# A fused transformer layer in fp32: the output projection's offset added in the second norm, and VectorE's loop end in attention set behind a pair's maxima

## What is computed

```python
x = _ln(src) * (1.0 + scale) + shift
q = (x @ Wq + bq) ... ; k = (x @ Wk + bk) ... ; v = (x @ Wv + bv) ...
scores = jnp.einsum('bhqd,bhkd->bhqk', q / math.sqrt(HEAD_DIM), k) + attention_bias
scores = jnp.where(src_mask, -jnp.inf, scores)
probs = jax.nn.softmax(scores, axis=-1)
ctx = jnp.einsum('bhqk,bhkd->bhqd', probs, v).transpose(0, 2, 1, 3).reshape(B, S, D)
x = x + (ctx @ Wo + bo)
h = _ln(x) * g2 + beta2
ff = _gelu2(h @ W1 + b1) @ W2 + b2
return x + ff
```

## Time and profile before

| | |
|---|---|
| median of 3 runs | 2465.89 us (2464.13 to 2466.8) |
| the profiled execution | 2472.93 us, its span 2471.1 us |
| mean granted TensorE clock | 0.988 |
| TensorE busy | 2363.4 us |
| VectorE busy | 1830.4 us |
| GpSimd busy | 1840.8 us |
| ScalarE busy | 1323.4 us |

### The profile page before, as it was taken

The page is one execution under the profiler, slowest core; times in us unless marked ns, Lnnn a source line. Parts: engine busy times, 40 slices in busy tenths (PEclk is TensorE's granted clock), DMA queues, the critical chain, the costliest instruction groups (busy, mean ns, idle before and its releaser), DMA issues.

```text
span 2471.1 us, 61234 instructions
## 1 busy us (share of the span) xinstructions
PE 2363.4 (96%) x21010; PEld 2234.2 (90%) x21010; DVE 1830.4 (74%) x2921; ACT 1323.4 (54%) x3663; POOL 1840.8 (74%) x1785
## 2 busy tenths in 40 slices
PE   4999999999999999987999999999989999999998
PEld 3888888888888888867999999999979999999998
DVE  4788888888888888777666666666577676777776
ACT  2566666566666666575555555555543333343332
POOL 3777777777777777778777777777896777767675
PEclk8999999999999999999999999999999999999999
DMA  7344444344434444333343434343465556555563
GB/s 241 109 134 134 139 140 134 110 134 139 139 115 137 135 139 136 102 90 122 147 159 136 161 144 154 141 161 146 159 219 170 185 181 188 184 183 187 170 196 125
DMA packets 288978, 372.26 MB, mean 151 GB/s; under 512 B 28544, under 2 KB 202752, under 8 KB 288768
## 3 DMA queue, kind: packets, MB, share of 16 engines
q1 hardware_dynamic: 288768, 369.57, 46.2%
HBM read 251.81 MB, written 117.70 MB: 150 GB/s over the span
## 4 chain that ended last, share of the span: by engine, by line
PE 85%; DVE 5%; issue 3%; POOL 3%; ACT 1%; DMA 1%; SPq 0%; DVEq 0%; POOLq 0%; ACTq 0%
PE up L1568 14%; PE up L1566 14%; PE up L1567 14%; PE turn L923 5%; PE psD L923 4%; PE psD L924 4%; PE psD L925 4%; PE turn L925 4%; PE turn L924 4%; PE psS L952 4%; PE psC L962 2%; PE psS L938 2%; PE turn L1566 2%; PE turn L1567 2%; PE turn L1568 2%
## 5 line engine op out<-in xcount | busy, mean ns | idle before, releaser
L1566 PE MATMUL up<-T,wc 128*128 128x256 f32 x1792 | 511.2, 285 | 14.7 <-DVE gu L1440 7.0
L1568 PE MATMUL up<-T,wc 128*128 128x256 f32 x1792 | 508.0, 283 | 0.0
L1567 PE MATMUL up<-T,wc 128*128 128x256 f32 x1792 | 505.4, 282 | 0.0
L597 POOL TENSOR_TENSOR s<-s,rinv 128x512 f32<-128x512 f32 x254 | 265.2, 1045 | 234.2 <-DVE rinv L791 231.7
L713 ACT ACTIVATE s<-s,nmx 128x128 f32<-128x128 f32 x1024 | 396.2, 394 | 5.5 <-issue 5.5
L1566 PE MATMUL up<-wc,gs 128*128 128x256 f32 x1280 | 360.2, 281 | 3.2 <-DVE gs L1523 3.2
L657 POOL TENSOR_TENSOR bias<-bias,mneg 128x512 f32<-128x512 f32 x256 | 351.8, 1394 | 13.7 <-DVE mneg L796 13.7
L1567 PE MATMUL up<-wc,gs 128*128 128x256 f32 x1280 | 359.9, 281 | 0.0
L1568 PE MATMUL up<-wc,gs 128*128 128x256 f32 x1280 | 359.8, 281 | 0.0
L1566 PEld LDWEIGHTS up<-T,wc 128*128 128x128 f32 x1792 | 339.3, 189 | 18.5 <-DVE gu L1440 8.4
L1567 PEld LDWEIGHTS up<-T,wc 128*128 128x128 f32 x1792 | 340.7, 190 | 0.0
(11 more groups left out here) (209 smaller groups left out, 7043.8 us busy)
## 6 DMA issues: line engine op xcount, KB each, us to landing
bias<-in_bias SPq DMA_DIRECT2D x128, 512.0 KB, 5.4
gated<-gu SPq DMA_DIRECT2D x128, 512.0 KB, 2.6
adab<-ada_rows SPq DMA_DIRECT2D x64, 512.0 KB, 5.5
gbuf<-gated SPq DMA_DIRECT2D x64, 512.0 KB, 3.9
gu<-gated SPq DMA_DIRECT2D x63, 512.0 KB, 3.9
xin<-in_x SPq DMA_DIRECT2D x32, 512.0 KB, 5.1
resid<-rout SPq DMA_DIRECT2D x64, 256.0 KB, 2.2
r<-resid SPq DMA_DIRECT2D x16, 1024.0 KB, 6.0
```

Source lines behind the costliest of these rows:

```text
L597: eng.tensor_tensor(s[:, b, heads, :], s[:, b, heads, :], rinv[:, b, heads].unsqueeze(2).to_broadcast([P, HG, S]), ALU.mult).then_inc(done, 1)
L1566: pe.matmul(out_ap, sh, mh, start=start, stop=False)
L1567: pe.matmul(out_ap, sh, ml, start=False, stop=False)
L1568: return pe.matmul(out_ap, sl, mh, start=False, stop=stop)
```

## The change

Four things are changed.

1. `bo` is no longer added to `rout`; the store waits for L806's result alone. `SecondNorm.add_bo` adds it to `r`, once per batch of a group: group 0 at t = 57 ahead of its statistics, group 1 at t = 64, its statistics now one step later (`on.end == 1`), group 2 in the first up group at j = 6 and 7, groups 3 to 15 at j = 4 (three) and 5 (one) of the up groups 1 to 13, behind c11. There the spread and the first two normalizations stand behind c11 as well. `bo` for the later groups is loaded by a DMA into `b2_bc` at the end of attention. As `resid` now lacks it, `bo` is added to b2 in the first group of `down`.
2. VectorE's loop end in attention lies between the halves of a b = 1 step, and the normalization of x, the first reciprocal and the spread belong to `second_half`, so that the branch follows the maxima.
3. In the last up group and the first of down, VectorE makes the combination of one weight unit and the sums of the first two gated units, which GpSimd made; GpSimd's other combinations stand later.
4. In the first up group the second half's transposes stand at j = 5.

```diff
+    def add_bo(self, dve, n, b):
+        at_least(dve, self.r_in, (n + 1) * DMA)
+        dve.tensor_tensor(self.of(n)[:, b, :], self.of(n)[:, b, :], self.bo[0 if isinstance(n, int) and n < 2 else 1], ALU.add).then_inc(self.bo_added, 1)
+
     def statistics(self, dve, n, b):
-        at_least(dve, self.r_in, (n + 1) * DMA)
+        at_least(dve, self.bo_added, n * self.NB + (b + 1))
...
+    def sums_early(self, dve, m):
+        at_least(dve, self.raw_in[self.place(m)], self.arrived(m))
+        combine(dve, slot(self.raw[self.place(m)]), B_TYPE, self.v_part, 0, self.v_sums)
...
             def store(t, b):
-                at_least(sp, bo_added, t + 1)
+                at_least(sp, r_ready, t + 1)
...
                 if on.end == 0:
+                    sp.wait_ge(v_done, B)
+                    sp.dma_start(second.bo[1], d["bo"].rearrange("(a f) -> a f", a=1).to_broadcast([P, DM])).then_inc(second.bo_in, DMA)
...
                 dve.tensor_tensor(rout[:, b, :], psD[0][:, :], norm.xres[:, slot, b, :], ALU.add).then_inc(r_ready, 1)
-                at_least(dve, r_ready, t + 1)
-                dve.tensor_tensor(rout[:, b, :], rout[:, b, :], bo_bc[:, :], ALU.add).then_inc(bo_added, 1)
...
                     for m in range(second.NB):
-                        second.statistics(dve, 1, m)
+                        second.add_bo(dve, 1, m)
...
+
+            def second_half(p, u, b, on):
+                t = p * 2 + b
                 if on.norm:
...
-            def second_half(p, u, b, on):
-                t = p * 2 + b
...
                 if on.end == -7:
                     for m in range(second.NB):
+                        second.add_bo(dve, 0, m)
+                    for m in range(second.NB):
                         second.statistics(dve, 0, m)
...
+                if on.end == 1:
+                    for m in range(second.NB):
+                        second.statistics(dve, 1, m)
...
                 first_half(first, first % UNROLL, 0, steady(0))
+                second_half(first, first % UNROLL, 0, steady(0))
+                first_half(first, first % UNROLL, 1, steady(1))
                 with dve.Fori(0, (last - first + 1) // UNROLL) as i:
-                    for m in range(2 * UNROLL):
+                    for m in range(1, 2 * UNROLL + 1):
...
         def turns_at(first):
-            return (2, 4) if first else (0, 2)
+            return (2, 5) if first else (0, 2)
...
-            return {1: 0, 2: 1, 4: 2, 5: 3}.get(j)
+            return {1: 0, 4: 2, 5: 3}.get(j)
...
-                if fixed(n) and n == LAST and j >= 6:
-                    sums(j - 6, j - 6)
...
             def before_down():
                 c22_u4(K - 1, 3)
-                weights.sums(pool, J + 4)
-                sums(2, 2)
                 gather(K - 2, 2)
                 gather(K - 1, 3)
+                sums(2, 2)
...
-                if first and j in (0, 1, 3):
-                    weights.sums(pool, J + (5, 6, None, 7)[j])
-                if first and j == 2:
-                    pool.wait_ge(b2_in, DMA)
+                if first and j < 4:
+                    weights.sums(pool, J + 4 + j)
+                if first and j == 4:
+                    pool.wait_ge(b2_in, 2 * DMA)
+                    pool.tensor_tensor(bb[:, :], bb[:, :], c1.rearrange("p i n -> p (i n)"), ALU.add).then_inc(bb_sum, 1)
+                    pool.wait_ge(bb_sum, 1)
                     pool.tensor_tensor(bb[:, H:], bb[:, H:], bb[:, 0:H], ALU.subtract).then_inc(bb_ready, 1)
...
                 if fixed(n) and n == LAST:
+                    if j == 3:
+                        weights.sums_early(dve, J + 1)
+                    if j >= 6:
+                        early_two(j - 6)
...
                     if first and j in (6, 7):
-                        norm.statistics(dve, n + 2, 2 * (j - 6))
-                        norm.statistics(dve, n + 2, 2 * (j - 6) + 1)
+                        dve.wait_ge(norm.bo_in, DMA)
+                        for b in range(2):
+                            norm.add_bo(dve, n + 2, 2 * (j - 6) + b)
+                        for b in range(2):
+                            norm.statistics(dve, n + 2, 2 * (j - 6) + b)
                     if not first and j in (5, 6):
                         norm.statistics(dve, n + 2, j - 3)
-                    if j == (7 if first else 6):
+                    if first and j == 7:
                         norm.spread(dve, n + 2)
-                    if not first and j == 7:
-                        norm.normalize(dve, n + 2, 0)
-                        norm.normalize(dve, n + 2, 1)
...
                 c11(k, j % 4)
+                if not first and has(n, 2):
+                    if j == 4:
+                        for b in range(3):
+                            norm.add_bo(dve, n + 2, b)
+                    if j == 5:
+                        norm.add_bo(dve, n + 2, 3)
+                    if j == 6:
+                        norm.spread(dve, n + 2)
+                    if j == 7:
+                        for b in range(2):
+                            norm.normalize(dve, n + 2, b)
```

More of the change, by code:

```diff
@@ L195, in __init__ @@
             sem("cols_in"), sem("expo_ok2"), sem("bn_done2"), sem("part_done2"), sem("var_ready2"), sem("rstd_ready2"), sem("hn_ready"))
+        self.bo_in, self.bo_added, self.bo = sem("bo_in"), sem("bo_added"), [None, None]
         self.xt_done, self.xt_copied, self.t_part, self.t_sums, self.t_hi, self.t_ready = (
@@ L287, in __init__ @@
         self.w_part, self.w_sums, self.w_hi, self.w_ready = sem("factor_part"), sem("factor_sums"), sem("factor_hi"), sem("factor_ready")
+        self.v_part, self.v_sums = sem("factor_part_v"), sem("factor_sums_v")
     def place(self, m):
@@ L314, in of, with count @@
         return raw[1] if piece else raw[0][:, 1:4, :]
+    def count(self, m):
+        return m - 1 if m > self.units + 1 else m
     def sums(self, pool, m):
         at_least(pool, self.raw_in[self.place(m)], self.arrived(m))
-        combine(pool, slot(self.raw[self.place(m)]), A_TYPE if m < self.units else B_TYPE, self.w_part, m, self.w_sums)
+        combine(pool, slot(self.raw[self.place(m)]), A_TYPE if m < self.units else B_TYPE, self.w_part, self.count(m), self.w_sums)
+    def sums_early(self, dve, m):
+        at_least(dve, self.raw_in[self.place(m)], self.arrived(m))
+        combine(dve, slot(self.raw[self.place(m)]), B_TYPE, self.v_part, 0, self.v_sums)
     def high(self, act, m, piece):
@@ L322, in high @@
         if piece:
-            at_least(act, self.w_sums, m + 1)
+            at_least(act, *((self.v_sums, 1) if m == self.units + 1 else (self.w_sums, self.count(m) + 1)))
         act.activation(self.wc[:, self.AT[m % self.units], 0, (RAW, COMBINED)[piece], :], self.of(m, piece), ACT.Copy).then_inc(self.w_hi, 1)
@@ L571, in attention_part @@
         pt_done, pt_copied, pv_done = sem("pt_done"), sem("pt_copied"), sem("pv_done")
-        ctx_hi, ctx_split, o_done, bo_added = sem("ctx_hi"), sem("ctx_split"), sem("o_done"), sem("bo_added")
+        ctx_hi, ctx_split, o_done = sem("ctx_hi"), sem("ctx_split"), sem("o_done")
         ident = norm.ident
@@ L911, in run_halves @@
                     for b in range(2):
+                        if p > last + 1:
+                            first_half(p, p % UNROLL, b, half(p, b, PAIRS))
                         if p > last + 1 or b:
-                            first_half(p, p % UNROLL, b, half(p, b, PAIRS))
-                        second_half(p, p % UNROLL, b, half(p, b, PAIRS))
+                            second_half(p, p % UNROLL, b, half(p, b, PAIRS))
             run_halves()
@@ L1080, in feed_part @@
         g_out = [sem(f"g_out{i}") for i in range(4)]
-        b2_in, bb_ready = sem("b2_in"), sem("bb_ready")
+        b2_in, bb_sum, bb_ready = sem("b2_in"), sem("bb_sum"), sem("bb_ready")
         g_in = [sem(f"g_in{i}") for i in range(4)]
@@ L1084, in feed_part @@
         g_first, g_sums = sem("g_first"), sem("g_sums")
+        early_part, early_sums = sem("early_part"), sem("early_sums")
         s_part, s_sums, s_hi, s_ready, acc_done = sem("s_part"), sem("s_sums"), sem("s_hi"), sem("s_ready"), sem("acc_done")
@@ L1217, in down @@
                     sp.wait_ge(s_ready, 4)
-                    sp.dma_start(b2_bc[:, :], d["b2"].rearrange("(a f) -> a f", a=1).to_broadcast([P, DM])).then_inc(b2_in, DMA)
+                    for t, name in ((b2_bc[:, :], "b2"), (c1.rearrange("p i n -> p (i n)"), "bo")):
+                        sp.dma_start(t, d[name].rearrange("(a f) -> a f", a=1).to_broadcast([P, DM])).then_inc(b2_in, DMA)
                 if first and j in (1, 3):
@@ L1294, in sums @@
                 pool.tensor_tensor(t[:, 5, :], t[:, 4, :], t[:, 1, :], ALU.subtract).then_inc(s_part, 1)
-                at_least(pool, s_part, k + 1)
+                at_least(pool, s_part, k - 1)
                 pool.tensor_tensor(t[:, 7, :], t[:, 2, :], t[:, 5, :], ALU.subtract).then_inc(s_sums, 1)
```

(10 more changed lines are left out.)

## The result

The changed kernel takes 2477.23 us (median of 11 runs, 2474.55 to 2483.4), the kernel before 2467.43 in the same sessions (11 runs, 2463.08 to 2475.41): ratio 1.0038, 95% interval 1.0026 to 1.0049. It is slower by about 10 us. The forecast was 2455 us with a range of 2443 to 2473, so the sign is wrong and the time lies 4 us outside.

A forecast was written before the change was run, and what follows sets the result against it. TensorE, busy 96%, was taken as the limit almost everywhere. -18.8 + 3.4 + 0 + 3.3 + 9.1 - 4 - 4 = -11.0 us took the profiled 2472.93 to 2461.9; less 7.0 for the median, 2455 us, range 2443 to 2473.

The forecast's parts named there:

- The loop end: Attention, VectorE's five taken branches: moved behind the maxima, the gap is covered; -18.8 us, bounds 0 and -18.8.
- a gap of 5.1 us that moves as it is: Attention's loop end: the gap keeps its size behind the maxima; the context's low part still ends 2.1 us before use.
- rival 3: Attention's loop ends: the gap costs the same behind the maxima, 18.8 us comes back, 2474 us; chance 0.10.
- Group 0: Second norm, additions ahead of its statistics: nothing covers the four while TensorE waits for v; +3.4 us (2.5 to 5.6).
- Group 2: First up group: the last two additions have no cover, the first two stand a unit earlier; +3.3 us (1 to 5.6).
- Steady groups: Groups 3 to 15, in up: four additions cost 4.2, less 2.5 idle and 0.8 slack, taken as 0.7; thirteen times, +9.1 us.
- the slack of 0.8: Up groups: the second pair of normalizations ends at 1343.16, their half's transposes start near 1344.0, so 0.8 us of lateness is free.
- The upper end of that term: Groups 3 to 15: 31 us, said to follow from 5.6 for four additions, at most 2.5 absorbed and slack gone elsewhere.
- The change over: Last up and first down group: work moved from GpSimd to VectorE gains -4 (0 to -6) and -4 (-12 to +2) us.
- From profile to median: Whole kernel: the median of three runs stood 7.0 us below the profiled execution, so 2461.9 became 2455 us.
- Slower: the additions spread: Up groups: additions pay 1.41 each and push GpSimd back 2.4; transposes wait 2.4 us a group, 31 not 9, 2477; chance 0.16.
- The up loop gets gaps of its own: VectorE's longer up loop falls on the wrong side: five taken branches at 3.8 us give +19, 2474 us; chance 0.04.

The follow-up runs named there:

- g2_one_column: The changed kernel with the additions of bo to groups 0 and 2 cut to one column each, instructions at their places; 2474.0 us (one run).
- g_no_adds_0_2: The changed kernel without the additions of bo to groups 0 and 2; 2487.2 us.
- b_no_adds: The changed kernel without the additions of bo to r in groups 3 to 15; 2458.3 us.
- e_stats_instead: The changed kernel with each addition of bo in groups 3 to 15 replaced by a one-operand bn_stats of the same 512 columns; 2463.1 us.
- after_again: The changed kernel once more, unaltered, timed over 12 runs; 2475.7 us, ratio 1.0041 to the kernel before.
- a_end_only: The kernel before with the loop end moved behind the maxima and nothing else; 2447.5 us, ratio 0.992.

## Why the prediction was wrong

- **The loop end: right in place and size.** The steps behind it are 15.7 to 16.1 us in four profiles. What failed was the picture of a gap of 5.1 us that moves as it is; it was 1.5. The wait from the branch to the next instruction is itself shorter at the new place (2.8 to 3.2 us against 4.0 to 5.3), and the maxima ahead of the branch cover about half of it. That made the move safer than I had it, and rival 3 (the gap costs the same) moot.
- **Group 0: +3.4 forecast, +4.2 (g2_one_column) to +6.1 (g_no_adds_0_2) measured.** TensorE's wait for v is 5.2 us, near the 5.4 forecast. Up starts 15.2 us earlier, against 15.4 forecast. That the two agree so well is in part luck: two of the four profiles of the changed kernel have attention's steps at 15.75, 3 us less in each, and without that the gain would be some 1.5 us smaller.
- **Group 2: +3.3 forecast, about 5.4 more in the first two groups.** 4.1 of it goes with the additions; where the other 1.3 comes from stays open. It did not show as a longer wait for r but for T, 4.1 us (1.7 with one column), whose low part stands behind them on VectorE. My list of what is late next ended at r.
- **Steady groups: the step that failed, "I take 0.7. Thirteen times: +9.1".** Measured +16.1 to +21.7, mean 18.8, so 1.24 to 1.67 a group. The price of an addition was close (1.10 against 1.05), and the slack of 0.8 was real: the stretch became 1.7 us longer and the transposes waited 0.94. Too large was what I let lateness be absorbed with. I counted all 2.5 us of VectorE's idle time, of which 2.1 were used, and took off 0.2 more for overlap. And I let the move behind c11 cost nothing; b_no_adds has it at 3.5 us in all, 0.27 a group. The additions alone cost 0.97 a group by the first profiles. The rest came with a new spread: groups that were 42.05 in every execution became 43.2 to 44.2, and differ from one execution to the next. That this is because VectorE has nothing left over (19.82 of 20.24 us) is likely, not shown. A trace of one execution of the kernel before could not show that spread.
- **The upper end of that term does not follow from its own words.** With 5.6 for four additions, 2.5 absorbed and no slack, 3.1 a group or 40 us would stand there, not 31; 31 is 13 times the 2.4 of the rival.
- **The change over: -4 and -4 forecast, near 0 and -0.7.** GpSimd's busy time in the last up group did fall, from 41.0 to 36.0 us, and VectorE's rose from 26.8 to 31.1; the group's length, cut alike, stayed at 45.8 to 45.9. High busy time of GpSimd was taken for the limit. TensorE's waits in these two groups name VectorE in both kernels, and none GpSimd: before, 4.8 us for the low part of weights (wc), 7.4 for that of gated units (gs) and 2.7 for c21 (gu); now 4.6, 6.0 and 2.3.
- **From profile to median.** I took 7.0 us off because the profiled execution was 7.0 above the median. The 7.0 was no property of profiling: the profiled execution is the shortest of e_stats_instead's ten and the longest of after_again's twelve, and the changed kernel's is its median run. In the one of before, down was in its middle length and the steps of attention in the longer, as in the changed kernel's. Without the 7.0 the same sum would have given 2462 us.
- **The rivals.** "Slower: the additions spread", with 0.16, is the nearest: 2.4 us a group and 2477 were its price. The total met it, 2477.23, but by luck: the groups had 1.24 to 1.67, and the two -4 and the 7.0 that did not come made up for what they lacked. "The up loop gets gaps of its own" did not happen here, though 248 more instructions ahead of it were enough to make it happen.

In sum, in place of -11.0: -15.2 in attention, +5.4 in the first two groups, +18.8 in the 13, about 0 in the last, -0.7 in the first of down: +8.3 us.

## What to carry to other kernels

An instruction that costs nothing on an engine with room is not free elsewhere. In attention, once the loop end was moved, the steps are as long with bo's 64 additions (a_end_only) as without them. In the second norm they cost over 20 us (4.2, 4.1 and at least 12.6), in places where VectorE was near full. When work is moved to an engine that is busy 16 of 18.5 us, do not count all of its idle time as room or round the remainder down, and ask for each instruction behind the new one (here T, p1c, r) who waits for it. Before calling an engine's busy time the limit, look for a wait that names it. And take the part of a change that pays by itself: the loop end alone gave all that there was.

## What the runs showed of the hardware

- At a taken branch of VectorE's loop in attention the next instruction comes 4.0 to 5.3 us later at one place of the branch and 2.8 to 3.2 at another; where the loop has no gap, 0.3. The idle time is what the work issued ahead of the branch leaves of it: 5.1 us behind seven short instructions, 1.5 behind maxima, 0.7 behind the same with an addition among them. So a loop end belongs behind long instructions.
- Where the body lies matters beside its length: a body of 304 instructions had no gap. The same body 248 instructions further had 2.8 to 3.0 us from each of five branches to the next instruction, and a second gap of 1.7 a few instructions on; some 20 us were lost over up. The instruction queue's packets (119 against 92) tell the two apart.
- A VectorE addition of 512 columns with two operands in SBUF and GpSimd additions take turns: 1.22 and 1.19 us, where VectorE's takes 0.68 and GpSimd's 0.74 undisturbed. A BATCH_NORM_STATS2 of the same width, with one operand, stays at 0.68.
- One program takes different lengths in different executions, in steps: a later unit of down 4.93, 4.98 or 5.04 us (586.5, 593.1 or 599.8 in all), a step of attention 15.75 or 15.84. TensorE's granted clock is at its full level (2.4 GHz) through later down in the profiles with 586.5, 593.1 and 599.8 alike. What chooses between them stays open; a median of six runs is uncertain by some 5 us (a_end_only's interval is 0.9902 to 0.9939).
